# A graph network kernel on one core: distance factors of four batches at a time, with right sides made by a VectorE shuffle

## The chip, the cores and the metric

The kernel runs on one NeuronCore of one Trainium2 chip. The metric is the device time in microseconds (us) of one execution; the other cores are idle.

## The reference, cut to what matters

There are 16 batches of a graph with 512 nodes and 128 features. The first layer computes, for each batch, a convolution branch and a neighbour branch, and joins them in a GRU-like cell. The neighbour branch is where the change lies:

```python
s = x @ w_se.T + b_se                                  # 512 x 3
sq = jnp.sum(s * s, axis=-1)
dist = sq[:, :, None] + sq[:, None, :] - 2.0 * jnp.einsum('bnd,bmd->bnm', s, s)
A = jnp.exp(-dist) * mask
msg = jax.nn.relu(x @ w_msg.T + b_msg)
x_nmp = jnp.einsum('bnm,bmd->bnd', A, msg)
```

The convolution branch is a 1x1 convolution, a 17-tap convolution along the nodes and batch norms. A layer norm follows, then a small grouped graph layer over the first 32 nodes of each batch and a second layer norm.

## The kernel before, in words

One program handles one batch in each step, b = 0 to 15. Step 0 is unrolled with the loading of the weights (`first`), step 1 is unrolled, steps 2 to 13 are a loop over v = 2, 3, 4, 5 with four steps a turn, and steps 14 and 15 are unrolled. Odd and even steps differ: the convolution is done for two batches together, so its first half lies in the odd steps and its second half in the even ones. All five engines run their own instruction order, written out by hand, and meet at semaphores.

The negated distance matrix of a batch is a product of two thin factors. `rows` (TensorE, line 723 on) multiplies `wrow` by the inputs of two batches, one in the upper and one in the lower 64 partitions of the bank `p_gh`. From it ScalarE makes `ab` (`rows_factor`, L1016), VectorE makes `val` (`rows_val`, L1365), ScalarE rounds it (`rows_high`, L1020) and VectorE makes `left` (`rows_left`, L1369). For each of the two batches `left` holds 24 rows of the left factor and 24 rows of the right factor. This chain runs once in each odd step, for the two batches that come next, eight times in all.

The four 128-row pieces of a distance matrix are taken by four matrix products with 24 rows each (`dist`), which sit in four different groups of 32 partitions. The factors must therefore stand in all four groups. SyncE copies them there from SBUF to SBUF (`spread_factors`, L653 to L657): six transfers for each batch and twelve in an odd step, in one queue with the loads of `xin` (L680), the stores (L694) and the loads of `adj` (L626). The product of an even step uses the second batch of the pair, and that of the odd step the first one.

In an odd step VectorE runs in this order: `gate_mid`, `keep_share`, `result` (the end of the step before), `rows_val`, `mask_low` (`am_l`), `msg_sum`, `neighbour_steps`, `inner` (L1379), `rows_left`, `x_low` (L1361), `inner_low` (`t_l`, L1384), `second_steps`, `stats`, `outer`, `msg_low`, `neighbours_low`, `moments`, `middle_low`, `outer_low`, `first_sums`, and four `mask` (L1417). In the even step there follow the gates and `result` (L1434, L1436), `second_sums` (L1460 to L1462) and the rest. TensorE's fourth stream of the convolution (`stream(4, p_outer)`) waits for `second_sums`; `neighbours_low` (L1480) of the even step waits for TensorE's neighbour product through ScalarE (`neighbours`, L1062).

## Time and profile before

| quantity | value |
|---|---|
| median of 3 runs | 356.47 us (356.42 to 356.6) |
| profiled execution | 355.94 us |
| its span | 354.1 us |
| TensorE busy | 335.1 us (95%) |
| VectorE busy | 315.9 us (89%) |
| ScalarE busy | 237.4 us (67%) |
| mean granted TensorE clock | 0.99 of full speed |

The profile gives for each instruction its engine, its line, its start and its length, and for an engine that stood idle what ended the wait. PE is TensorE, DVE is VectorE, ACT is ScalarE, POOL is GpSimd, SPq is SyncE's queue. Two instructions of one engine may overlap a little, since one is filled while the one before drains.

### The profile page before, as it was taken

The numbers are of one execution on the slowest core, as the hardware profiler recorded it, in microseconds if no ns is written. First come the engines' busy times: TensorE is split into PE (matmuls) and PEld (weight loads), VectorE is DVE, ScalarE is ACT, GpSimd is POOL, SyncE is SP. The second block draws the span as 40 slices with busy tenths as digits, with TensorE's granted clock in tenths as the row PEclk, the third lists the DMA queues.
The fourth block names the chain that finished last, engine by engine and source line by source line (L and its number), as shares of the span: only waits on it lengthen the run. The fifth ranks groups of instructions, "written<-read, shape, count | busy, mean of one in ns | idle before, by whom it ended". The sixth has DMA issues, their size and how long they took to land. (4 is left out here: it accounts for less than half of the span.)

```text
span 354.1 us, 6242 instructions
## 1 busy us (share of the span) xinstructions
PE 335.1 (95%) x1769; PEld 273.2 (77%) x1769; DVE 315.9 (89%) x553; ACT 237.4 (67%) x409; POOL 94.4 (27%) x151
## 2 busy tenths in 40 slices
PE   5989999999999999999999999999999999999880
PEld 1577678987889688977998688968897798867570
DVE  2999999999999999999999999999999999896732
ACT  4382675748856696758674885669684886976760
POOL 4750001614050503231050506050222206052022
PEclk9999999999999999999999999999999999999996
DMA  6914331514153212604161404412260415301102
GB/s 197 310 23 126 103 118 47 168 31 149 24 145 109 99 52 64 210 0 148 39 205 30 148 17 109 149 67 81 56 203 15 148 33 156 107 26 37 30 2 60
DMA packets 31289, 34.01 MB, mean 96 GB/s; under 512 B 5111, under 2 KB 18463, under 8 KB 31271
## 3 DMA queue, kind: packets, MB, share of 16 engines
q1 hardware_dynamic: 30150, 33.49, 31.2%
q10 hardware_dynamic: 1120, 0.30, 0.4%
q8 instruction: 8, 0.13, 0.2%
q14 instruction: 11, 0.08, 0.1%
HBM read 24.85 MB, written 4.46 MB: 83 GB/s over the span
## 5 line engine op out<-in xcount | busy, mean ns | idle before, releaser
L1320 POOL TENSOR_TENSOR base<-mv,vscale 128x4 f32<-128x4 f32 x16 | 7.0, 437 | 230.9 <-DVE mv L1449 224.1
L715 PE MATMUL p_outer<-t_h,w_h 128*128 128x344 f32 x131 | 41.0, 328 | 0.0
L715 PE MATMUL p_outer<-t_h,w_l 128*128 128x344 f32 x131 | 40.3, 322 | 0.5 <-DVE w_l L1527 0.5
L1417 DVE TENSOR_TENSOR am<-am,adj 128x512 f32<-128x512 f32 x64 | 39.8, 682 | 0.0
L1583 DVE TENSOR_TENSOR am_l<-am,am_h 128x2048 fp32r<-128x2048 f32 x15 | 34.3, 2287 | 1.8 <-ACT am_h L1172 1.8
L715 PE MATMUL p_middle<-t_h,w_h 128*128 128x344 f32 x90 | 28.6, 329 | 0.6 <-DVE rz L1533 0.6
L1172 ACT ACTIVATE am_h<-am 128x2048 fp32r<-128x2048 f32 x15 | 28.5, 1901 | 0.0
L715 PE MATMUL p_middle<-t_h,w_l 128*128 128x344 f32 x90 | 28.0, 322 | 0.0
L715 PEld LDWEIGHTS p_outer<-t_h,w_h 128*128 128x128 f32 x131 | 24.3, 188 | 2.1 <-ACT t_h L1029 0.4
L1131 ACT ACTIVATE yoo<-yn,nb,rs 128x128 f32<-128x128 f32 x63 | 25.9, 483 | 0.0
L715 PEld LDWEIGHTS p_outer<-t_h,w_l 128*128 128x128 f32 x131 | 24.4, 189 | 1.1 <-DVE w_l L1527 0.8
L715 PE MATMUL ring<-am_h,m_h 128*128 128x512 f32 x60 | 24.2, 404 | 0.6 <-DVE mt L1406 0.6
L715 PE MATMUL p_outer<-t_l,w_h 128*128 128x344 f32 x131 | 24.7, 322 | 0.0
L1062 ACT ACTIVATE n_h<-ring 128x512 fp32r<-128x512 f32 x16 | 9.5, 596 | 22.2 <-PE ring L715 22.2
L715 PE MATMUL ring<-am_h,m_l 128*128 128x512 f32 x60 | 23.5, 392 | 0.0
L1076 ACT ACTIVATE gtn<-gtn,vec 128x512 f32<-128x512 f32 x15 | 10.9, 724 | 17.6 <-DVE gtn L1423 17.6
L1329 POOL TENSOR_TENSOR nmr<-mv,rs 128x4 f32<-128x4 f32 x16 | 21.1, 1322 | 2.7 <-issue 0.9
L715 PEld LDWEIGHTS p_outer<-t_l,w_h 128*128 128x128 f32 x131 | 21.6, 188 | 0.0
L1327 POOL TENSOR_TENSOR rs<-base,cst 128x5 f32<-128x5 f32 x16 | 21.0, 1314 | 1.3
L715 PEld LDWEIGHTS p_middle<-t_h,w_h 128*128 128x128 f32 x90 | 16.8, 189 | 0.8 <-issue 0.8
L1049 ACT ACTIVATE am<-p_outer 128x512 f32<-128x512 f32 x14 | 8.4, 599 | 12.9 <-PE p_gh L715 12.9
L715 PE MATMUL p_middle<-t_l,w_h 128*128 128x344 f32 x90 | 16.9, 322 | 0.0
(381 smaller groups left out, 1012.1 us busy)
## 6 DMA issues: line engine op xcount, KB each, us to landing
adj<-adjT SPq DMA_DIRECT2D x64, 256.0 KB, 3.4
xpad<-xT SPq DMA_DIRECT2D x17, 256.0 KB, 3.1
out<-yoo SPq DMA_DIRECT2D x16, 256.0 KB, 2.3
crossed<-left SPq DMA_DIRECT2D x31, 48.0 KB
left<-left SPq DMA_DIRECT2D x30, 48.0 KB
right<-left SPq DMA_DIRECT2D x30, 48.0 KB
wc<-w_c SPq DMA_DIRECT2D x2, 384.0 KB, 6.8
wraw<-g_w SPq DMA_DIRECT2D x1, 640.0 KB
```

The lines of the kernel that those rows point to most:

```text
L715: return nc.tensor.matmul(out_, w, x, start=start, stop=stop, skip_group_check=True)
L1049: A(am[:, c, :], banks[c][:], ACT.Exp).then_inc(s_e[c], 1)
L1062: A(n_h[:], R_NMP[:], ACT.Copy).then_inc(s_nh, 1)
L1076: A(nn, tt, ACT.Tanh, bias=vec[:, V_IN:V_IN + 1]).then_inc(s_nn, 1)
L1131: return A(yo[q][:, c, :], rows_, ACT.Identity, bias=nb[:, c:c + 1], scale=rs[:, c:c + 1])
L1172: A(am_h[:], am[:], ACT.Copy).then_inc(s_amh, 1)
L1320: TT(base[:, 0:CH], mv[:, :, 1], vscale[:, 0:CH], ALU.mult)
L1327: TT(rs[:], base[:], cst[:, C_MH:C_MH + CH + 1], ALU.pow).then_inc(s_rs, 1)
L1329: TT(nmr[:, 0:CH], mv[:, :, 0], rs[:, 0:CH], ALU.mult)
L1417: TT(am[:, c, :], am[:, c, :], adj[:, c, :], ALU.mult).then_inc(s_am[c], 1)
L1583: TT(am_l[:], am[:], full(am_h[:]), ALU.subtract).then_inc(s_aml, 1)
```

## The change

The factors get 30 rows of 15 and 15, so that both sides of a batch lie in one group of 32 partitions, the right side being the left one with its halves exchanged. One chain now makes the factors of up to four batches: batches 0 and 1 at the start, 2 and 3 in step 1, and 4 to 7, 8 to 11 and 12 to 15 in steps 3, 7 and 11. For the last two batches of such a group TensorE reads a copy `xr` of the inputs, loaded by SyncE in the steps with v = 2. In steps 5, 9 and 13 the chain is gone. The right sides are made by a `stream_shuffle` on VectorE, which writes `crossed` behind `x_low`. SyncE spreads seven transfers for each batch into `lefts` and `rights`, which exist twice: fourteen in steps 1, 3, 7 and 11, and seven in each of the steps with v = 4 and v = 5. In the start the right side of batch 0 is copied by ScalarE, and the bias column `brow` comes in one transfer.

The core of the diff:

```diff
-KD = 24
+KROW = 15
+KD = 2 * KROW
...
-            left.append((k, 1.0, 0.0, low))
-            right.append((None, 0.0, -1.0, 0))
-    for low in (0, 1):
-        for k in range(3):
-            left.append((None, 0.0, 1.0, 0))
-            right.append((k, -1.0, 0.0, low))
-    return left, right
+    first, second = [], []
+    for k in range(3):
+        first += [(k, 0.0, 1.0, 0), (k, 0.0, 1.0, 0), (k, 0.0, 1.0, 1), (k, -1.0, 0.0, 0), (k, -1.0, 0.0, 1)]
+        second += [(k, 0.0, 1.0, 0), (k, 0.0, 2.0, 1), (k, 0.0, 1.0, 1), (None, 0.0, 1.0, 0), (None, 0.0, 1.0, 0)]
+    return first + second, []
...
@@ -148,8 +140,9 @@
         adj = sb("adj", [128, CH, N])
         rows2 = sb("rows2", [128, 2 * N]); ab = rows2[:, 0:N]; val = rows2[:, N:2 * N]; val_h = sb("val_h", [128, N], fp32r)
-        left = sb("left", [128, N], fp32r)
-        crossed = sb("crossed", [128, N], fp32r); left2 = sb("left2", [128, N], fp32r); right2 = sb("right2", [128, N], fp32r)
+        left = sb("left", [128, N], fp32r); crossed = val
+        lefts = [sb(f"lefts{p}", [128, N], fp32r) for p in range(2)]; rights = [sb(f"rights{p}", [128, N], fp32r) for p in range(2)]
+        xr = sb("xr", [128, 2, N])
         he = sb("he", [128, 2, 2 * W3 + 2])
...
-                rows_l, rows_r = full(left[64 * q:64 * q + KD, :]), full(left[64 * q + 32:64 * q + 32 + KD, :])
-                sp.dma_start(full(crossed[64 * q:64 * q + KD, :]), rows_r).then_inc(s_right[q], 16)
-                sp.dma_start(full(crossed[64 * q + 32:64 * q + 32 + KD, :]), rows_l).then_inc(s_right[q], 16)
-                for at in (64 - 64 * q, 96 - 64 * q):
-                    sp.dma_start(full(left2[at:at + KD, :]), rows_l).then_inc(s_right[q], 16)
-                    sp.dma_start(full(right2[at:at + KD, :]), rows_r).then_inc(s_right[q], 16)
+            def spread_factors(v, event=None):
+                g, p = v % 4, v % 2
+                rows_l, rows_r = full(left[32 * g:32 * g + KD, :]), crossed[32 * g:32 * g + KD]
+                for h in range(4):
+                    if h != g:
+                        sp.dma_start(full(lefts[p][32 * h:32 * h + KD, :]), rows_l).then_inc(s_right[p], 16)
+                if event is not None:
+                    after(sp, s_crossed, event)
+                for h in range(4):
+                    sp.dma_start(full(rights[p][32 * h:32 * h + KD, :]), rows_r).then_inc(s_right[p], 16)
             sp.wait_ge(s_left, 1)
-            sp.dma_start(full(crossed[0:KD, :]), full(left[32:32 + KD, :])).then_inc(s_right[0], 16)
-            spread_factors(1)
+            spread_factors(1, 1)
             sp.wait_ge(s_zero, 3)
             for g, q in itertools.product(range(NG), range(2)):
                 load_group(g, q)
...
                     sp.dma_start(xin[:, (v + 3) % 4, :], xT[(b + 3) % B, :, :]).then_inc(s_x[(v + 3) % 4], 16)
-                if v % 2 and before(b, B - 2):
-                    after(sp, s_left, n.pair(1))
+                if v == 2:
+                    after(sp, s_rows, n.quad(0))
                     for q in range(2):
-                        spread_factors(q)
+                        sp.dma_start(xr[:, q, :], xT[b + 4 + q, :, :]).then_inc(s_xr, 16)
+                if v == 3 or static(b, 1):
+                    after(sp, s_left, n.quad(0)); after(sp, s_d, n(1))
+                    spread_factors(v + 1, n.quad(0))
+                    spread_factors(v + 2)
+                elif not isinstance(b, int):
+                    if v != 2:
+                        after(sp, s_d, n(0))
+                        spread_factors(v + 2)
                 if not static(b, 1):
...
-            def rows(v):
+            def row_group(g, x_):
+                return mm(p_gh[32 * g:32 * g + 32, :], wrow[:], x_)
+            def rows(v, extra=False):
                 for q in range(2):
-                    last = mm(p_gh[64 * q:64 * q + 64, :], wrow[:], xin[:, (v + q) % 4, :])
+                    last = row_group((v + q) % 4, xin[:, (v + q) % 4, :])
+                if extra:
+                    for q in range(2):
+                        last = row_group(2 + q, xr[:, q, :])
                 last.then_inc(s_rows, 1)
...
-                at, other = 64 * (v % 2), 64 - 64 * (v % 2)
-                for c, (lhs, rhs, row) in enumerate(((left, crossed, at), (crossed, left, at + 32),
-                                                     (left2, right2, other), (left2, right2, other + 32))):
-                    last = mm(banks[c][:], lhs[row:row + KD, D * c:D * c + D], rhs[row:row + KD, :])
+                for c in range(CH):
+                    h, p = (v + c) % 4, v % 2
+                    lhs, rhs = left if c == 0 else lefts[p], rights[p]
+                    last = mm(banks[c][:], lhs[32 * h:32 * h + KD, D * c:D * c + D], rhs[32 * h:32 * h + KD, :])
                 last.then_inc(s_d, 1)
...
                         pe.wait_ge(s_x[(v + k) % 4], x_count(n, v, k))
-                    after(pe, s_ghb, n(0))
-                    rows(v + 1)
+                    if v == 3 or static(b, 1):
+                        after(pe, s_ghb, n(0))
+                        if v == 3:
+                            after(pe, s_xr, n.quad(-2) * 32)
+                        rows(v + 1, v == 3)
                     after(pe, s_xh, n(3)); after(pe, s_xl, n(3))
                     after(pe, s_w0, n.pair(0)); after(pe, s_pq, n.pair(0)); after(pe, s_e[0], n(1))
                     conv1(q, p_middle)
...
                     g_pe.combine(pe, mm)
-                if more:
-                    after(pe, s_val, n.pair(1))
+                if v == 3 or static(b, 1):
+                    after(pe, s_val, n.quad(0))
                 after(pe, s_ghb, n(0)); gate(p_gh, "n", 2, xb_h, xb_l, True, True).then_inc(s_gx, 1)
                 turn(n)
...
                 if more:
-                    after(pe, s_left, n.pair(1)); after(pe, s_right[0], n.pair(1) * 96 - 80)
+                    after(pe, s_left, n.quad(0)); after(pe, s_right[0], n.pair(0) * 112)
...
-            def rows_high(n, k):
-                after(act, s_val, n.pair(k + 1)); after(act, s_left, n.pair(k))
-                A(val_h[:], val, ACT.Copy).then_inc(s_valh, 1)
+            def rows_factor(at, e):
+                after(act, s_rows, e); after(act, s_val, e - 1)
+                A(ab[at], p_gh[at, :], ACT.Identity, bias=rowb[at, 0:1], scale=cst[at, C_ROW:C_ROW + 1]).then_inc(s_ab, 1)
+            def rows_high(at, e):
+                after(act, s_val, e); after(act, s_left, e - 1)
+                A(val_h[at, :], val[at], ACT.Copy).then_inc(s_valh, 1)
             def first_conv(n, k, slot, source):
                 after(act, s_c1, n(k + 1)); after(act, s_f, n.pair(0))
...
                 act.dma_start(vec[:], vecs[:, :]).then_inc(s_vec, 16)
-                act.dma_start(wrow[:], w_rows[:, :]).then_inc(s_wrowd, 16)
+                act.dma_start(wrow[:], w_rows[:, 0:32]).then_inc(s_wrowd, 16)
                 act.dma_start(wmsg[:], w_msg[:, :]).then_inc(s_wmsgd, 16)
-                for q in range(2):
-                    act.dma_start(brow[64 * q:64 * q + 64, :], b_rows[:, :]).then_inc(s_brow, 16)
+                act.dma_start(brow[:], b_rows[0:32, :].unsqueeze(0).broadcast_to([4, 32, 1])).then_inc(s_brow, 16)
                 act.dma_start(bmsg[:], b_msg[:, :].to_broadcast([128, D])).then_inc(s_bmsg, 16)
...
                 act.wait_ge(s_rowb, 1)
-                act.wait_ge(s_rows, 1)
-                A(ab, p_gh[:], ACT.Identity, bias=rowb[:, 0:1], scale=cst[:, C_ROW:C_ROW + 1]).then_inc(s_ab, 1)
-                act.wait_ge(s_val, 1)
-                A(val_h[:], val, ACT.Copy).then_inc(s_valh, 1)
+                rows_factor(slice(0, 64), 1)
+                rows_high(slice(0, 64), 1)
                 middle_high(o)
                 act.wait_ge(s_mt, 1)
                 A(m0, mt[:], ACT.Relu).then_inc(s_m0, 1)
+                act.wait_ge(s_crossed, 1)
+                A(rights[0][0:32, :], crossed[0:32], ACT.Copy).then_inc(s_cross0, 1)
                 act.wait_ge(s_wsum, 2)
                 A(w3_h[:], u3, ACT.Copy).then_inc(s_whi, 1)
...
-            def rows_val(n, k):
-                after(dve, s_ab, n.pair(k + 1)); after(dve, s_valh, n.pair(k))
-                STT(val, p_gh[:], brow[:, 0:1], ab, ALU.add, ALU.mult).then_inc(s_val, 1)
-            def rows_left(n, k):
-                after(dve, s_valh, n.pair(k + 1)); after(dve, s_d, n(2 * k + 1))
-                STT(left[:], full(val_h[:]), cst[:, C_ROW + 2:C_ROW + 3], val, ALU.mult, ALU.add).then_inc(s_left, 1)
+            def rows_val(at, e, done):
+                after(dve, s_ab, e); after(dve, s_valh, e - 1); after(dve, s_d, done)
+                STT(val[at], p_gh[at, :], brow[at, 0:1], ab[at], ALU.add, ALU.mult).then_inc(s_val, 1)
+            def rows_left(at, e, done):
+                after(dve, s_valh, e); after(dve, s_d, done)
+                STT(left[at, :], full(val_h[at, :]), cst[at, C_ROW + 2:C_ROW + 3], val[at], ALU.mult, ALU.add).then_inc(s_left, 1)
+            def rows_crossed(at, e):
+                nc.vector.stream_shuffle(crossed[at], full(left[at, :]), MIRROR).then_inc(s_crossed, 1)
             def neighbour_steps(n):
...
                 last.then_inc(s_t04, 1)
-                rows_val(o, 0)
-                rows_left(o, 0)
+                rows_val(slice(0, 64), 1, 0)
+                rows_left(slice(0, 64), 1, 0)
+                dve.wait_ge(s_left, 1)
+                rows_crossed(slice(0, 64), 1)
                 dve.wait_ge(s_bmsg, 16)
                 msg_sum(z, 0, FIRST_MSG)
                 dve.wait_ge(s_w2d[1], 16)
...
                     neighbour_steps(n)
                     inner(n)
-                    rows_left(n, 0)
+                    if v == 3 or static(b, 1):
+                        rows_left(part_of(v), n.quad(0), n(1))
+                        after(dve, s_left, n.quad(0))
                     x_low(v, n, 3)
+                    if v == 3 or static(b, 1):
+                        rows_crossed(part_of(v), n.quad(0))
                     inner_low(n)
                     second_steps(n)
                 else:
```

## Rows read from the trace of the kernel before

**Rows 1.** The page, part 1: busy time of each engine over the span.

```profile
PE 335.1 (95%) x1769; PEld 273.2 (77%) x1769; DVE 315.9 (89%) x553; ACT 237.4 (67%) x409; POOL 94.4 (27%) x151
```

**Rows 2.** One period: window, length, busy PE, PEld, DVE, ACT, POOL, clock, DMA share.

```profile
100.00:138.72 38.72, 38.66 (x211) 32.55 (x207) 37.03 (x63) 27.75 (x45) 9.76 (x15) 1.00 0.32 98
```

**Rows 3.** Timeline of VectorE, step 7 into step 8 (start us, length us).

```profile
169.69 0.75 DVE L1369 SCALAR_TENSOR_TENSOR left<-val_h,cst,rows 128x512 fp32r<-128x512 f32 x1
170.35 0.69 DVE L1361 TENSOR_TENSOR x_l<-xpad,x_h 128x512 fp32r<-128x512 f32 x1
170.96 0.90 DVE L1384 TENSOR_TENSOR t_l<-yy,t_h 128x712 fp32r<-128x712 f32 x1
...
178.69 2.48 DVE L1417 TENSOR_TENSOR am<-am,adj 128x512 f32<-128x512 f32 x4
...
183.28 0.69 DVE L1434 SCALAR_TENSOR_TENSOR yy<-rz,gtn 128x512 f32<-128x512 f32 x1 [0.19 <-ACT gtn L1076]
184.07 0.69 DVE L1436 TENSOR_TENSOR yy<-yy 128x512 f32<-128x512 f32 x1
...
185.65 0.57 DVE L1462 SCALAR_TENSOR_TENSOR wc<-p_outer,prm,wc 128x344 f32<-128x344 f32 x1
```

**Rows 4.** Timeline of TensorE at the fourth stream of step 8.

```profile
185.94 0.60 PE L794 MATMUL ring<-cst,yy 128*128 128x128 f32 x4
186.29 0.41 PE L715 MATMUL p_outer<-t_h,w_h 128*128 128x344 f32 x1
```

**Rows 5.** Timeline of VectorE in step 4, where a neighbour product is read.

```profile
115.10 0.69 DVE L1480 TENSOR_TENSOR n_l<-ring,n_h 128x512 fp32r<-128x512 f32 x1 [0.52 <-ACT n_h L1062]
```

**Rows 6.** Timeline of TensorE at the row products of step 5.

```profile
121.38 1.08 PE L715 MATMUL p_gh<-xpad,wrow 128*64 128x512 f32 x4
122.39 0.51 PE L715 MATMUL p_middle<-x_h,wc_h 128*128 128x512 f32 x1
```

**Rows 7.** Timelines of step 5: ScalarE, VectorE and TensorE, a line each.

```profile
122.74 0.72 ACT L1076 ACTIVATE gtn<-gtn,vec 128x512 f32<-128x512 f32 x1 [0.56 <-DVE gtn L1423]
123.37 0.76 ACT L1016 ACTIVATE rows<-p_gh,rowb,cst 128x512 f32<-128x512 f32 x1
124.03 1.90 ACT L1172 ACTIVATE am_h<-am 128x2048 fp32r<-128x2048 f32 x1
...
131.09 0.80 ACT L1029 ACTIVATE t_h<-yy 128x712 fp32r<-128x712 f32 x1
...
125.96 2.29 DVE L1583 TENSOR_TENSOR am_l<-am,am_h 128x2048 fp32r<-128x2048 f32 x1
...
129.93 1.13 DVE L1379 SCALAR_TENSOR_TENSOR yy<-he 128x712 f32<-128x712 f32 x1
...
132.25 0.89 DVE L1384 TENSOR_TENSOR t_l<-yy,t_h 128x712 fp32r<-128x712 f32 x1
...
132.15 0.32 PE L715 MATMUL p_outer<-t_h,w_h 128*128 128x344 f32 x1
```

**Rows 8.** A small VectorE instruction of the start.

```profile
40.86 0.15 DVE L1571 TENSOR_SCALAR dg<-dg 106x8 f32<-106x8 f32 x1
```

**Rows 9.** Step 5: SyncE's queue, the DMA engines by stretch, TensorE at the distances.

```profile
135.60 0.71 SPq L657 DMA_DIRECT2D right<-left  x1
136.36 0.71 SPq L653 DMA_DIRECT2D crossed<-left  x1
...
137.00:137.20 0.20, 0.20 (x3) 0.20 (x2) 0.20 (x1) 0.10 (x1) 0.00 (x0) 1.00 0.72 174
...
138.45 0.50 PE L715 MATMUL p_outer<-crossed,left 24*128 24x512 f32 x1
```

**Rows 10.** Timelines of the start: ScalarE, VectorE, TensorE.

```profile
18.10 0.85 ACT L1101 ACTIVATE w_h<-gtn 128x768 fp32r<-128x768 f32 x1 [3.61 <-DVE gtn L1520]
...
22.38 0.96 DVE L1530 TENSOR_TENSOR w_l<-gtn,w_h 128x768 fp32r<-128x768 f32 x1 [0.23 <-ACT w_h L1106]
...
24.89 1.20 PE L715 MATMUL p_middle<-t_h,w_h 128*128 128x344 f32 x6 [0.64 <-DVE rz L1533]
```

More of the change, by code:

```diff
@@ L86, in constants @@
     c[:, C_ID:C_ID + D] = np.eye(D)
-    for side, rows in enumerate(dist_rows()):
-        for r, (_, alpha, beta, low) in enumerate(rows):
-            for b in range(2):
-                c[64 * b + 32 * side + r, C_ROW:C_ROW + 3] = alpha, beta, -low
+    for r, (_, alpha, beta, low) in enumerate(dist_rows()[0]):
+        for g in range(4):
+            c[32 * g + r, C_ROW:C_ROW + 3] = alpha, beta, -low
     c[:, C_ONE] = 1
@@ L1609, in odd @@
                 result(n, -1)
-                if more:
-                    rows_val(n, 0)
+                if v == 3 or static(b, 1):
+                    rows_val(part_of(v), n.quad(0), n(1))
                 if not more:
```

41 lines of the change are left out of this document (20 added, 21 removed).

## The prediction

> **What bounds the kernel now.** I read the page first. TensorE is busy for 95% of the span and VectorE for 89% [rows 1], so TensorE looks like the bound, and a change that takes work from TensorE looks like a gain. The busy time by stretch corrects this. In one period of two steps, 38.72 us, TensorE is busy for 38.66 us and VectorE for 37.03 us [rows 2]. VectorE has 1.7 us left in a period, and part of that are gaps that a dependent instruction leaves behind itself. Both engines are full.
>
> The timelines then show which of the two holds the other, and where. From the writing of `left` in step 7 to the last of `second_sums` in step 8, VectorE's instructions follow each other without a wait for TensorE; the only named wait is 0.19 us for ScalarE, which itself follows from VectorE [rows 3]. The last `second_sums` starts at 185.65 and ends at 186.22. TensorE has its four transposes at 185.94, which take 0.35 us from start to start, and begins its fourth stream at 186.29 [rows 4]. That stream waits for `second_sums`, so VectorE is on time there by less than 0.1 us. What VectorE gets later before that place, TensorE gets later too. In the other direction VectorE waits 0.52 us for the neighbour product of the even step [rows 5]. There the clocks of the two are set together again, so a reserve that VectorE has won before it isn't carried past it. The bound is a loop through both: VectorE from the even step's neighbour product to `second_sums`, and TensorE from there to the next neighbour product.
>
> **The change part by part.**
>
> *TensorE, removed.* The row products occupy TensorE from 121.38 to 122.39, 1.0 us [rows 6]. Eight groups become five: steps 5, 9 and 13 lose theirs, so TensorE has 3 x 1.0 = 3.0 us less to do. In steps 3, 7 and 11 four products of 32 columns stand where two of 64 stood. A product has two records here, and 4 records are done in 1.08 us, so two column groups run beside each other; I take four to do the same, at no cost. The upper bound is that only two do: 1.0 us more in three steps.
>
> *The distance products.* 30 rows instead of 24 in the same four row groups: no cost, since the columns stay at 512.
>
> *Steps 5, 9 and 13, what the gain is worth.* The chain into the first stream of the odd step is: the candidate's tanh at 122.74, `ab` at 123.37, `am_h` at 124.03 on ScalarE, `am_l` at 125.96 on VectorE as soon as `am_h` is done, `inner` at 129.93, `t_h` at 131.09 to 131.89, TensorE at 132.15 [rows 7]. Without `ab`, `am_h` can start when the tanh ends, at 123.46: 0.57 us earlier. `rows_val` lies under `am_h` and gives nothing more. So `t_h` ends at 131.32, and TensorE, which would be ready 1.0 us earlier, at 131.15, starts at about 131.35: it gains 0.8 us. VectorE also drops `left`, and its `t_l` moves from 132.25 to the end of `t_h`, 0.9 us, so it isn't what limits here. Value: 0.8 us for each of the three; bounds 0.57 (only the chain's part) and 1.0 (all of TensorE's). Sum: -2.4 us, between -1.7 and -3.0.
>
> *Steps 1, 3, 7 and 11, what VectorE gets.* All of the old chain stays, and two things are added on VectorE between `left` and `t_l`: a wait for `left`'s own semaphore ahead of `x_low`, and the shuffle. `x_low` now starts 0.09 us before `left` has ended [rows 3]. A dependent pair with a wait starts 0.10 us after the end of the first (L1434 and L1436 in the same rows), so the wait costs up to 0.2 us; I take 0.15, and the lower bound is 0. The trace has no shuffle. The nearest row is `x_low`, also 512 elements a partition in fp32, with 0.61 us from start to start; `left` has 0.66. The shuffle's permutation must be loaded as well, by a small instruction; a small instruction of VectorE takes 0.15 us [rows 8], of which some may be overlapped. I take 0.70 us for both, between 0.60 and 0.95. Together 0.85 us, between 0.60 and 1.15. The Trainium skill, VectorE: DVE Perf Modes, section The DRAIN you can't avoid, says that a semaphore between two VectorE instructions costs nothing extra; the rows above show 0.2 us between the two cases, and by the rule the sum of this prediction would be about 0.8 us instead of 1.6. The same page, section The perf-mode tier table, gives a shuffle about 2400 ns for 2048 elements in its only mode, from which 512 elements would be an estimated 0.60 us.
>
> Nothing covers these 0.85 us. Behind them stand `t_l`, the steps of the convolution, four masks at 178.69, the gates and `second_sums`, each at once behind the other [rows 3], and TensorE's fourth stream has no reserve [rows 4]. So each of the four periods gets 0.85 us longer: +3.4 us, between +2.4 and +4.6. `t_l` itself is still just in time for TensorE.
>
> *The start.* The same wait and shuffle stand in `first`, ahead of the sums of the taps, for which ScalarE waits 3.61 us; the later VectorE work there holds TensorE, which waits 0.64 us at 24.89 [rows 10]. One wait of VectorE for ScalarE, 0.23 us, takes up a part. Cost +0.6 us of 0.85, between 0.35 and 0.9. ScalarE's copy of batch 0's right side lies in those 3.61 us. The bias column comes in one transfer instead of two; I give it nothing.
>
> *SyncE's transfers.* One starts 0.76 us after the other. The sixth, the last one that the odd step's product waits for, starts at 135.60, the DMA engines still move data for it from 137.0 to 137.2 and I take 137.4 as its end, and TensorE takes the factors at 138.45 [rows 9]. With 0.76 us more the seventh lands at about 138.1, 0.3 us in time. The four right sides wait for the shuffle, but three left sides are issued first, 2.3 us, and the shuffle is done about 1.5 us after `left`. Behind the fourteen transfers stand the store and the `adj` loads of the step, later by two transfers, 1.5 us, and their masks stand a whole step further on; in the steps with v = 4 and 5 the seven transfers stand in an idle queue. Cost nothing; if the queue's cover is gone, see the rival.
>
> Sum: +0.6 + 3.4 - 2.4 = +1.6 us. The profiled execution took 355.94 us with a span of 354.1, and would take 357.5; the median of the runs lies 0.53 us above it, so 356.47 + 1.6 = 358.1 us.
>
> **The rivals.** 0.2% is 0.7 us, and that is about what a measurement can tell from no change.
>
> *VectorE's additions are cheap.* The shuffle and the wait cost 0.60 us, 0.35 in the start, and steps 5, 9 and 13 give 0.9 each: 0.35 + 2.4 - 2.7 = 0.05 us, no change, 356.5 us. For it: `x_low`'s own 0.61 us. Against it: the gap behind a wait. Chance 22%.
>
> *TensorE alone sets the time.* If VectorE has a reserve of 0.85 us before `second_sums` that I don't see, its additions are hidden and the 3.0 us stand: 353.5 us. For it: 95% against 89% [rows 1]. Against it: under 0.1 us between the engines at the fourth stream. It decides once the reserve is above the cost of the additions. Chance 13%.
>
> *The right sides come late.* If a transfer of 30 rows costs more of SyncE's queue than one of 24, the seventh lands later. In proportion to the rows it would be 0.95 us each; the seventh would land at about 139.3 and hold TensorE by 0.85 us, beside VectorE's delay and not on top of it. It decides above that: at 1.15 us each, TensorE is 2.05 us late, 1.2 us more than VectorE, four times: 358.1 + 4.8 = 362.9 us. Chance 7%.
>
> *The four narrow products don't run together.* TensorE is 1.0 us later in three steps; 0.85 us of it lie beside VectorE's delay, so it adds 0.15 x 3: 358.6 us. Chance 8%. The Trainium skill, TensorEngine Tiling (Array Packing), section Tiling Modes, counts four independent tiles of 128x32, which speaks against this rival; only the two column groups are seen here.
>
> **How the numbers follow.** My forecast has 50%. Its own range is 356.9 to 359.6, from the bounds of the additions and of the gain. Slower by over 0.2%: most of the forecast (45%), late right sides and serial products: 60%. Within 0.2%: the cheap additions and the low end of the forecast: 24%. Faster: TensorE alone and the best end of the cheap case: 16%. The range of 8 in 10 is 355.1 to 359.8: it leaves out TensorE alone and most of the late right sides.
>
> **What would show it.** In the profile after, VectorE's `t_l` in step 7 starts about 0.85 us later behind `left` than 1.27 us, and `second_sums` ends after TensorE's transposes, with TensorE waiting about 0.8 us there in steps 2, 4, 8 and 12. The period with step 5 is 0.8 us shorter, with TensorE's first stream waiting for `t_h`. The row products of step 7 take 1.0 us. I am wrong if the fourth stream starts right behind the transposes in step 8, if the shuffle takes clearly more or less than 0.7 us, or if TensorE waits at the distances of step 3.

## The result, and the profile after

The kernel after takes 364.38 us (median of 4 runs) against 356.45 us before; the ratio is 1.0154, with an interval of 1.0084 to 1.0225. Here and below the medians are over all executions, while the ratios leave disturbed ones out. I had forecast 358.1 us and a range up to 359.8. The direction was right, the time lies outside the range. The profiled execution took 363.85 us with a span of 362.0, 7.9 us more than before.

The page of the kernel after, first the busy time [rows 1], then two rows of the 40 slices:

```profile
PE 335.5 (93%) x1769; PEld 273.5 (76%) x1769; DVE 316.8 (88%) x557; ACT 234.6 (65%) x404; POOL 91.0 (25%) x151
...
PE   4498998999998999999999999999999999999880
...
PEclk9789999999999999999999999999999999999996
```

TensorE's busy time is the same (335.1 us before) although it has less to do. Its first two slices have lost time (4 and 4 tenths, 5 and 9 before), while the third is nearly full, and the granted clock fell to 7 and 8 tenths in the second and third (9, which is 90% or more, before). To place the rest I took, in both traces, the start of each batch's four distance products on TensorE. Their differences are the delay so far:

| stretch, from which products to which | after minus before, us | forecast |
|---|---|---|
| span's start to batch 0 (25.05 for 18.34) | +6.7 | +0.6 |
| batch 0 to 1 | +0.04 | (in the row above) |
| batch 1 to 3, with step 1 | +1.53 | +0.85 |
| batch 3 to 5, with step 3 | +1.53 | +0.85 |
| batch 5 to 7, with step 5 | -0.91 | -0.8 |
| batch 7 to 9, with step 7 | +0.83 | +0.85 |
| batch 9 to 11, with step 9 | -0.92 | -0.8 |
| batch 11 to 13, with step 11 | +0.81 | +0.85 |
| batch 13 to 15, with step 13 | -0.99 | -0.8 |

The middle came out nearly as forecast. The start did not, and steps 1 and 3 cost nearly twice what I gave them. At batch 15 the delay is 8.6 us, of which the span keeps 7.9: from there to the end the kernel after takes 42.4 us and the one before 43.2, and no run shows why.

**The start.** VectorE, GpSimd and TensorE of the kernel after, timelines (start us, length us):

```profile
10.71 0.27 DVE L1533 TENSOR_SCALAR rowb<-brow,cst 128x1 f32<-128x1 f32 x1 [3.31 <-DMA brow<-b_rows]
10.90 0.70 DVE L1537 TENSOR_TENSOR he<-he 128x534 f32<-128x534 f32 x1
11.64 0.63 DVE L1540 SCALAR_TENSOR_TENSOR yy<-he 128x356 f32<-128x356 f32 x1
12.19 2.05 DVE L1537 TENSOR_TENSOR he<-he 128x534 f32<-128x534 f32 x1
14.27 2.12 DVE L1540 SCALAR_TENSOR_TENSOR yy<-he 128x356 f32<-128x356 f32 x1
...
12.05 1.61 POOL L1329 TENSOR_TENSOR yoo<-wc 128x640 f32<-128x640 f32 x1 [4.02 <-DMA wc<-w_c]
13.74 2.15 POOL L1331 TENSOR_TENSOR gtn<-yoo,wc 128x768 f32<-128x768 f32 x1
...
16.44 5.78 PE L731 MATMUL p_outer<-yy,wc 128*128 128x344 f32 x12 [4.98 <-DVE yy L1540]
```

For comparison, VectorE and TensorE of the kernel before:

```profile
8.25 0.27 DVE L1504 TENSOR_SCALAR rowb<-brow,cst 128x1 f32<-128x1 f32 x1 [0.56 <-DMA brow<-b_rows]
...
11.17 3.75 PE L715 MATMUL p_outer<-yy,wc 128*128 128x344 f32 x12 [0.42 <-DVE yy L1511]
...
18.34 0.70 PE L715 MATMUL ring<-crossed,left 24*128 24x512 f32 x2 [0.53 <-issue]
```

The bias column `brow`, now one transfer, lets VectorE wait 3.31 us for a tiny instruction, and everything of the start is queued behind it. Of two equal pairs of `he` and `yy`, the convolution's first terms, the first takes 0.70 and 0.63 us, the second, beside GpSimd's tap sums, 2.05 and 2.12. TensorE stands idle for 4.98 us. Then its twelve products take 5.78 us where they took 3.75 before. The windows of the kernel after show the clock over this time (window, length, busy PE, PEld, DVE, ACT, POOL, granted clock, DMA share):

```profile
11.00:14.00 3.00, 0.47 (x5) 0.28 (x3) 2.97 (x3) 0.77 (x1) 1.87 (x2) 0.96 1.04 391
14.00:16.40 2.40, 0.00 (x0) 0.00 (x0) 2.37 (x3) 0.00 (x0) 2.32 (x2) 0.50 0.75 279
16.40:18.00 1.60, 1.56 (x3) 1.08 (x4) 0.90 (x2) 0.92 (x2) 1.60 (x1) 0.50 0.11 42
...
19.50:20.50 1.00, 1.00 (x3) 0.65 (x2) 1.00 (x2) 0.53 (x1) 0.93 (x1) 0.50 0.23 55
20.50:22.00 1.50, 1.50 (x6) 0.94 (x5) 1.47 (x3) 0.92 (x3) 0.86 (x2) 0.97 0.23 55
```

While TensorE is idle the clock goes from 2.4 to 1.2 GHz (0.50 of full speed) and stays there until about 20.5. The 6.7 us are therefore, to 0.1 us, 2.46 for the column (10.71 instead of 8.25), 2.81 for the slow pair, 2.03 for the slow products, less 0.53 that TensorE had idle ahead of its first distance products before.

**Step 7.** VectorE [rows 3] and SyncE's queue [rows 9] of the kernel after, and TensorE at the distance products:

```profile
178.62 0.74 DVE L1394 SCALAR_TENSOR_TENSOR left<-val_h,cst,rows 128x512 fp32r<-128x512 f32 x1
179.48 0.69 DVE L1386 TENSOR_TENSOR x_l<-xpad,x_h 128x512 fp32r<-128x512 f32 x1
180.10 0.01 DVE L1398 LOAD_MASK_SELECT rows<-left  x1
180.10 0.74 DVE L1398 STREAM_SHUFFLE rows<-left 128x512 f32<-128x512 f32 x1
180.73 0.89 DVE L1413 TENSOR_TENSOR t_l<-yy,t_h 128x712 fp32r<-128x712 f32 x1
...
179.38 2.52 SPq L662 DMA_DIRECT2D lefts<-left  x3
181.94 3.25 SPq L666 DMA_DIRECT2D rights<-rows  x4
...
186.74 0.47 PE L731 MATMUL p_outer<-rights,left 30*128 30x512 f32 x1 [0.51 <-issue]
...
195.39 0.57 DVE L1491 SCALAR_TENSOR_TENSOR wc<-p_outer,prm,wc 128x344 f32<-128x344 f32 x1
...
196.01 0.43 PE L731 MATMUL p_outer<-t_h,w_h 128*128 128x344 f32 x1
```

and TensorE at the same distance products of the kernel before:

```profile
177.13 0.50 PE L715 MATMUL p_outer<-crossed,left 24*128 24x512 f32 x1
```

From `left` to `t_l` 2.11 us pass instead of 1.27. The 0.84 us more are 0.63 for the shuffle, start to start, and 0.20 for the wait ahead of `x_low` (0.86 from `left` to `x_l`, 0.66 before); loading the permutation takes 0.01. That is the term as I sized it. But the row at 186.74 is a second finding: TensorE stood idle for 0.51 us ahead of the distance products, a wait that the profile gives only as "issue". They start 8.12 us after `left`; before they started 7.44 us after it (177.13 after 169.69), and TensorE was never idle there. And in step 8 `second_sums` ends at 195.96 and TensorE starts its fourth stream at 196.01, right behind transposes at 195.57. I had written that this would make me wrong: the wait of 0.8 us for VectorE isn't there, since TensorE is late already. So would a wait of TensorE at the distances of step 3, and there the idle time is larger still:

```profile
109.54 0.47 PE L731 MATMUL p_outer<-rights,left 30*128 30x512 f32 x1 [1.38 <-issue]
```

**Steps 5 and 7, what was removed.** TensorE's row products in step 7 [rows 6], and the first stream of step 5 [rows 7], of the kernel after:

```profile
168.97 0.62 PE L731 MATMUL p_gh<-xpad,wrow 128*32 128x512 f32 x2
168.99 0.62 PE L731 MATMUL p_gh<-xr,wrow 128*32 128x512 f32 x2
169.43 0.60 PE L731 MATMUL p_gh<-xpad,wrow 128*32 128x512 f32 x2
169.44 0.60 PE L731 MATMUL p_gh<-xr,wrow 128*32 128x512 f32 x2
169.97 0.50 PE L731 MATMUL p_middle<-x_h,wc_h 128*128 128x512 f32 x1
...
140.26 0.80 ACT L1054 ACTIVATE t_h<-yy 128x712 fp32r<-128x712 f32 x1 [0.60 <-DVE yy L1408]
...
141.11 0.19 PEld L731 LDWEIGHTS p_outer<-t_h,w_h 128*128 128x128 f32 x1 [0.43 <-ACT t_h L1054]
141.11 0.43 PE L731 MATMUL p_outer<-t_h,w_h 128*128 128x344 f32 x1
```

The four narrow products run beside each other and take 1.0 us together, as the two did. In step 5 the first stream starts as soon as `t_h` is done at 141.06; its weight load (PEld) had waited 0.43 us for `t_h`, so the chain through ScalarE limits there, as forecast.

### The profile page after: what moved, and what is told of

The parts are those of the page before. It is cut to its first block and busy times, and to the rows that moved or that the text cites. A ratio compares the mean times of both kernels' runs of the same rounds, so it can differ in the third digit from the quotient of the medians.

```text
span 362.0 us, 6268 instructions
## 1 busy us (share of the span) xinstructions
PE 335.5 (93%) x1769; PEld 273.5 (76%) x1769; DVE 316.8 (88%) x557; ACT 234.6 (65%) x404; POOL 91.0 (25%) x151
## 5 line engine op out<-in xcount | busy, mean ns | idle before, releaser
L1354 POOL TENSOR_TENSOR nmr<-mv,rs 128x4 f32<-128x4 f32 x16 | 19.8, 1235 | 2.7 <-issue 0.9
```

The source lines that it names most:

```text
L1354: TT(nmr[:, 0:CH], mv[:, :, 0], rs[:, 0:CH], ALU.mult)
```

## The experiments

All were compared with the kernel before on the same chip. In the table, "step 7" is the stretch from batch 7's distance products to batch 9's in the profiled execution, less the 38.55 us of the kernel before; "left to dist" is from the start of `left` in step 7 to batch 8's distance products. The column "start to batch 0" is read from one execution of each kernel. It differs by 2 us among kernels whose column came in time (17.31 to 19.29), for a reason given at c2.

| kernel | median, us | ratio to before | start to batch 0 | step 7 | left to dist |
|---|---|---|---|---|---|
| before | 356.5 to 356.9 | 1 | 18.34 | 0 | 7.44 |
| after | 364.38 | 1.0154 (1.0084 to 1.0225) | 25.05 | +0.83 | 8.12 |
| a1, two brow transfers | 356.90 | 1.0019 (0.9987 to 1.0051) | 17.78 | +0.83 | 8.12 |
| b1, before with one | 363.67 | 1.0172 (1.0125 to 1.0218) | 24.20 | +0.02 | |
| b2, b1 issued early | 359.32 | 1.0034 (0.9999 to 1.0068) | 21.76 | | |
| c3, b1 without the repeat | 362.15 | 1.0117 (1.0072 to 1.0163) | 24.86 | | |
| c2, b1 with GpSimd held | 360.27 | 1.0088 (1.0057 to 1.0119) | 22.08 | | |
| c1, after, rowb later | 358.80 | 1.0057 (1.0018 to 1.0097) | 17.02 | +0.84 | |
| a3, wait covered | 357.81 | 1.0036 (1.0013 to 1.0059) | 18.00 | +0.69 | 8.12 |
| a4, six transfers | 357.36 | 1.0017 (0.9994 to 1.0040) | 19.00 | +0.86 | 7.70 |
| d1, no shuffle | 356.44 | 0.9996 (0.9960 to 1.0032) | 17.62 | +0.68 | 8.13 |
| g1, no shuffle, six | 354.07 | 0.9926 (0.9904 to 0.9948) | 17.31 | -0.01 | 7.39 |
| g2, wait covered, six | 356.68 | 0.9999 (0.9979 to 1.0019) | 19.29 | +0.61 | 7.45 |
| f1, halves by SyncE | 354.95 | 0.9955 (0.9938 to 0.9971) | 19.18 | +0.16 | 7.39 |

### The bias column

**a1.** The kernel after with the column's loading of before.

```diff
-act.dma_start(brow[:], b_rows[0:32, :].unsqueeze(0).broadcast_to([4, 32, 1])).then_inc(s_brow, 16)
+for q in range(2):
+    act.dma_start(brow[64 * q:64 * q + 64, :], b_rows[:, :]).then_inc(s_brow, 16)
```

> The kernel after, with the bias column brow loaded in two transfers of 64 rows as before, and nothing else. Theory 1, the single broadcast transfer lands late and the whole start slides behind it: VectorE's rowb starts again near 8.3 us with a wait of about 0.9, its he and yy take 0.7 and 0.6 instead of 2.05 and 2.12, the first distance products start near 19.0 to 19.4 (before 18.34, after 25.05), and the kernel takes 358 to 359 us. Rival, the start is late because of the shuffle, the copy of batch 0's right side and the changed order there, and the transfer is only another thing to wait for: the first distance products stay above 23 us and the kernel takes 363 to 364 us.

Measured: 356.90 us, no difference from before that can be told, and the first distance products at 17.78 us. The rival falls: shuffle, ScalarE's copy and the new order of the start cost nothing up to batch 0's products; at batch 1's this kernel is 0.55 us behind the one before. The time, 1 to 2 us under what I expected, also says that the rest of the change is nearer to no change than to my +1.6.

**b1.** The kernel before with one transfer of the column.

```diff
-for q in range(2):
-    act.dma_start(brow[64 * q:64 * q + 64, :], b_rows[:, :]).then_inc(s_brow, 16)
+act.dma_start(brow[:], b_rows[:, :].unsqueeze(0).broadcast_to([2, 64, 1])).then_inc(s_brow, 16)
```

> The kernel before, with brow loaded by one transfer that repeats 64 rows twice, and nothing else. Theory 1: the start alone gets longer, the first distance products at 22 to 25 us instead of 18.34, and the kernel takes 360 to 363 us. Rival, the transfer is harmless: within 0.3 us of the kernel before. If the distance products are late by the lateness of rowb alone (about 2.5 us), and VectorE's he and yy keep their 0.7 and 0.6 us, then what made them 1.4 us longer each in the kernel after was not this transfer.

Measured: 363.67 us. All batches from the first to the last are 5.9 us late (5.86 at batch 0, 5.91 at batch 15), so the column alone, without anything else of the change, gives a start as late as that of the kernel after, to 0.85 us. VectorE and TensorE of b1:

```profile
10.49 0.27 DVE L1503 TENSOR_SCALAR rowb<-brow,cst 128x1 f32<-128x1 f32 x1 [3.09 <-DMA brow<-b_rows]
...
12.71 1.97 DVE L1510 SCALAR_TENSOR_TENSOR yy<-he 128x356 f32<-128x356 f32 x1
...
14.74 6.64 PE L715 MATMUL p_outer<-yy,wc 128*128 128x344 f32 x12 [3.42 <-DVE yy L1510]
```

The column is late by 2.24 us, one slow `yy` adds 1.33, and the products at the lower clock 2.89. Taken the other way, from the kernel after to a1, the column gives 7.3 us at batch 0, 6.7 at batch 15 and 7.5 in the medians.

**c2.** b1, and GpSimd waits.

```diff
 nc.gpsimd.tensor_copy(u2[:, G3 - 1:G3, :], wc2[:, TAPS - 2:TAPS - 1, :])
+pool.wait_ge(s_t04, 1)
```

> b1_one_brow, with GpSimd's tap sums held until VectorE's second yy is done. In b1_one_brow the second yy took 1.97 us instead of 0.63, beside GpSimd's first sum. Theory, the two slow each other: yy takes 0.63 again, and TensorE's p_outer<-yy starts 1.3 us earlier, at 13.4 instead of 14.74; the kernel is 1 to 2 us shorter than b1_one_brow if the later tap sums hold nobody. Rival, yy was slow for another reason (late data, the DMA engines): it keeps its 1.97 us. If TensorE's idle time of 3.42 us, now about 2.1, is also what its granted clock fell after (0.69 in the stretch from 10 to 20 us), the twelve products that took 6.64 us instead of 3.75 get shorter as well.

Measured: 360.27 us. In this run `rowb` itself came later (11.08 for 10.49), and yet TensorE began earlier:

```profile
11.08 0.27 DVE L1504 TENSOR_SCALAR rowb<-brow,cst 128x1 f32<-128x1 f32 x1 [3.68 <-DMA brow<-b_rows]
...
13.30 0.63 DVE L1511 SCALAR_TENSOR_TENSOR yy<-he 128x356 f32<-128x356 f32 x1
...
13.99 5.27 PE L715 MATMUL p_outer<-yy,wc 128*128 128x344 f32 x12 [2.73 <-DVE yy L1511]
```

`yy` takes 0.63 us with GpSimd standing still, so what made b1's `yy` slow is contention between the two engines. The products took 5.27 us instead of 6.64, after a shorter idle time. The span is 1.9 us shorter than that of b1, within the 1 to 2 us expected.

Which of the two starts first decides. GpSimd's first tap sum starts when its operand `wc`, the convolution's weights, has landed, at another time in each execution. In a4, where the column came in time (8.26), it did so ahead of `yy`:

```profile
10.09 1.79 POOL L1337 TENSOR_TENSOR yoo<-wc 128x640 f32<-128x640 f32 x1 [1.76 <-DMA wc<-w_c]
...
10.52 1.85 DVE L1548 SCALAR_TENSOR_TENSOR yy<-he 128x356 f32<-128x356 f32 x1
```

The same holds over all fourteen traces: the `he` or `yy` that starts 0.05 to 0.55 us behind a GpSimd sum takes 1.85 to 2.12 us, and a `yy` that starts 0.18 us or more ahead of it keeps its 0.63 to 0.64. In a4, f1 and g2 `yy` came second, and their batch 0 stands at 19.0 to 19.3 us instead of 17.3 to 18.3. So the slow pair is not a fixed price of the late column; the late column moved `he` and `yy` behind GpSimd's start.

**c1.** The kernel after, one transfer, but `rowb` and its wait behind the two pairs of `he` and `yy`.

```diff
-dve.wait_ge(s_brow, 16); dve.wait_ge(s_cst, 16)
-TS(rowb[:], brow[:], cst[:, C_ROW:C_ROW + 1], cst[:, C_ROW + 1:C_ROW + 2], ALU.mult, ALU.add).then_inc(s_rowb, 1)
...
 last.then_inc(s_t04, 1)
+dve.wait_ge(s_brow, 16); dve.wait_ge(s_cst, 16)
+TS(rowb[:], brow[:], cst[:, C_ROW:C_ROW + 1], cst[:, C_ROW + 1:C_ROW + 2], ALU.mult, ALU.add).then_inc(s_rowb, 1)
```

> The kernel after, with its single broadcast transfer of brow kept, but VectorE's rowb and the wait for brow moved behind the two he and yy, so that the late column no longer stands ahead of them in VectorE's queue. Theory 1, the late column costs what it does only because VectorE's queue stands still behind it: yy's end returns to about 10.9 us, TensorE starts p_outer<-yy near 11.2 instead of 16.44, the first distance products start at 18.5 to 19.5 us, and the kernel takes 357 to 358.5 us. Rival, the late values of the row products themselves hold the start: the first distance products stay above 22 us and the kernel takes over 361.

Measured: 358.80 us, and the first distance products at 17.02 us, earlier than in any other kernel. The late column costs what it does because an in-order queue stands behind it; it is not needed itself until later. By batch 1 c1 is 0.87 us behind the kernel before. The median lies 0.3 us above what I expected. The profiled execution took 362.18 us: the granted clock was 0.55 from 340 to 350 us, and the part behind batch 15's products took 46.7 us instead of the 42.5 of a1, so those 4 us say nothing about the column.

**c3 and b2.** What makes the one transfer late? c3 is the kernel before with one transfer of 128 rows from a column of 128 values, b2 is b1 with the transfer issued right behind `vec`.

```diff
-for q in range(2):
-    act.dma_start(brow[64 * q:64 * q + 64, :], b_rows[:, :]).then_inc(s_brow, 16)
+act.dma_start(brow[:], b_rows[:, :]).then_inc(s_brow, 16)
```

```diff
+act.dma_start(brow[:], b_rows[:, :].unsqueeze(0).broadcast_to([2, 64, 1])).then_inc(s_brow, 16)
 act.dma_start(wrow[:], w_rows[:, :]).then_inc(s_wrowd, 16)
 act.dma_start(wmsg[:], w_msg[:, :]).then_inc(s_wmsgd, 16)
-act.dma_start(brow[:], b_rows[:, :].unsqueeze(0).broadcast_to([2, 64, 1])).then_inc(s_brow, 16)
```

> The kernel before, with brow loaded by one plain transfer of 128 rows from a column of 128 values, so without the repeat. Theory, what delays the column is one transfer of 128 rows of 4 bytes where two of 64 stood: rowb waits about 3.1 us as in b1_one_brow and the kernel takes 360 to 364 us. Rival, the repeat in the source delays it: rowb waits 0.6 us, and the time is that of the kernel before.

> b1_one_brow, with the one broadcast transfer of brow issued second on ScalarE's queue, right behind vec (at about 1.2 us instead of 2.14), ahead of wrow and wmsg. In b1_one_brow the column was there at 10.4 us, 8.3 us after its issue. If such a transfer has a long time of its own, it lands about 8 us after its issue again, rowb starts near 9.5 us, and the kernel takes 360 to 362 us. Rival, it is late because it meets the loads of the weights and of x on the same DMA engines, and issued ahead of them it finds the engines free: rowb starts at 8.3 us or before, and the kernel takes 356.5 to 357.5 us.

Measured: 362.15 and 359.32 us. In c3 the first distance products start at 24.86, as late as with the repeat, but `rowb` now waits last for the transfer of `cst`, the constants that SyncE loads:

```profile
10.45 0.27 DVE L1503 TENSOR_SCALAR rowb<-brow,cst 128x1 f32<-128x1 f32 x1 [3.54 <-DMA cst<-consts]
```

`cst` took 7.8 us from issue to landing, 5.4 before, and `brow` 6.7 us, where the two took 4.7 and 5.5. In b2 `rowb` starts at 9.37, close to the 9.5 of a transfer with a long time of its own, but again it is `cst` that came last. b2's time lies between the two that I had expected. So taking the repeat away does not bring the start back, although the column itself was there sooner after its issue (6.7 us for 8.3 in b1), and an earlier place in the queue gets back about 1.1 us of VectorE's wait. `cst` was late as well in c3, b2 and b1 (7.8, 6.6 and 6.0 us), but not in c2 and in the kernel after (5.3). Why one transfer of 128 four-byte rows is late, and at times its neighbour, no run shows; this stays open.

### VectorE's additions and the transfers

**a3.** a1 with the wait and the shuffle later.

```diff
 rows_left(part_of(v), n.quad(0), n(1))
-after(dve, s_left, n.quad(0))
 x_low(v, n, 3)
-rows_crossed(part_of(v), n.quad(0))
+after(dve, s_left, n.quad(0))
 inner_low(n)
+rows_crossed(part_of(v), n.quad(0))
```

> a1_two_brow with VectorE's wait for its own left, and the shuffle, moved behind x_low and inner_low in steps 1, 3, 7 and 11, so that two other instructions cover the wait. Theory 2, VectorE's additions cost 0.63 us for the shuffle and 0.2 us for the wait ahead of it, and both delay second_sums: from left's start to t_l's start 1.9 us instead of 2.1 and the kernel 0.4 to 0.8 us shorter than a1_two_brow. Rival, in these steps the right sides' transfers decide: they start 1.2 us later here, so steps 1 and 3 get longer by up to 1.2 us each, and the kernel is 0.5 to 2 us longer than a1_two_brow.

Measured: 357.81 us, 1.0036; against a1 no gain can be told in the medians. In the profile step 7 costs 0.69 us instead of 0.83, and the distance products still come 8.12 us after `left`. The rival did not come true: the transfers started no later, because three left sides cover the later shuffle.

**a4.** a1 with ScalarE writing the own group's right side, six transfers instead of seven.

```diff
 for h in range(4):
-    sp.dma_start(full(rights[p][32 * h:32 * h + KD, :]), rows_r).then_inc(s_right[p], 16)
+    if own or h != g:
+        sp.dma_start(full(rights[p][32 * h:32 * h + KD, :]), rows_r).then_inc(s_right[p], 16)
...
+A(rights[0][g:g + 32, :], crossed[g:g + 32], ACT.Copy).then_inc(s_cross0, 1)
```

> a1_two_brow, where in steps 1, 3, 7 and 11 ScalarE copies the right side of the batch's own row group in place of one of the seven SyncE transfers, so that six transfers stand ahead of the odd step's distance products. Theory 3, the seventh transfer lands late where TensorE stood idle before the distance products (1.38 us in step 3, 0.51 in step 7): steps 1 and 3 get 0.5 to 0.8 us shorter each, steps 7 and 11 stay, and the kernel is 1 to 1.6 us shorter than a1_two_brow. Rival, the seventh transfer is hidden and ScalarE's copy of about 0.7 us lies in the way: the same time or up to 1 us more.

Measured: 357.36 us, no gain over a1 where I had expected 1 to 1.6 us. TensorE's idle time ahead of the distance products is gone in all four steps (7.68 to 7.74 us after `left`), but only step 3 got shorter, from +1.37 in a1 to +0.82; step 7 kept +0.86. As an explanation of the whole, theory 3 falls.

**d1.** a1 without the shuffle and its wait (an excerpt; the transfers of the right sides read rows that the shuffle of the start has written, from a buffer of their own).

```diff
-after(dve, s_left, n.quad(0))
 x_low(v, n, 3)
-rows_crossed(part_of(v), n.quad(0))
```

> a1_two_brow without the shuffle and without the wait ahead of it in steps 1, 3, 7 and 11; the right sides of every later batch are copies of the first shuffle's rows, so this kernel leaves out the mirroring and computes other distances. SyncE has the same fourteen transfers, and they wait only for left. Theory 2, VectorE's additions cost about 0.83 us in each of these four steps and hide nothing: 3 to 3.5 us shorter than a1_two_brow, 353.5 to 354 us, and steps 1 and 3 lose their extra 0.3 to 0.5 us as well because the right sides leave earlier. Rival, the transfers decide in these steps: only 1 us shorter or less. If the whole comes to less than 2.8 us shorter than the kernel before, something else in the change costs too.

Measured: 356.44 us; I had expected 353.5 to 354. This was the run that overturned my account: VectorE has 0.83 us less to do in each of four steps, and step 7 still costs 0.68. VectorE, SyncE and TensorE of d1:

```profile
171.17 0.75 DVE L1395 SCALAR_TENSOR_TENSOR left<-val_h,cst,rows 128x512 fp32r<-128x512 f32 x1
...
172.43 0.90 DVE L1414 TENSOR_TENSOR t_l<-yy,t_h 128x712 fp32r<-128x712 f32 x1
...
171.94 2.52 SPq L662 DMA_DIRECT2D lefts<-left  x3
174.50 3.25 SPq L666 DMA_DIRECT2D rights<-crossed  x4
...
179.30 0.47 PE L731 MATMUL p_outer<-rights,left 30*128 30x512 f32 x1 [0.63 <-issue]
```

`left` to `t_l` is 1.26 us again, but the seven transfers leave `left` as late as ever, and the distance products come 8.13 us after it. Seven transfers give 8.12 or 8.13 in step 7 of after, a1, a3 and d1 alike, whatever VectorE does. The kernel before needs 7.44; the difference, 0.68, is what the step costs in d1.

**g1.** So there are two delays side by side. g1 takes both away: d1 with a4's copy.

> d1_no_shuffle and a4_own_right together: no shuffle and no wait on VectorE in steps 1, 3, 7 and 11 (the mirroring is left out, the right sides are copies of the first shuffle's rows), and ScalarE writes the own group's right side, so that six transfers stand ahead of the odd step's distance products. Revised theory: two delays of about the same size lie side by side in each of these steps, VectorE's additions (0.83 us) and the seventh transfer with its larger pieces (the distance products start 8.12 us after left in every kernel with seven transfers, 7.44 before the change), and the later one counts; taking away one gives little, both together give 0.7 to 0.8 us a step: the distance products start 7.4 to 7.5 us after left, the kernel takes 353 to 354 us, about 3 us less than the kernel before. Rival, there is a third thing that costs in these steps: no better than d1_no_shuffle, 356.4 us.

Measured: 354.07 us, ratio 0.9926. Step 7 costs nothing (-0.01) and the distance products start 7.39 us after `left`. Over both kinds of periods: the removed row products give 0.89 us in step 5, and steps 7 and 11 take back nothing. Only step 3 still waits, 0.84 us for its right sides:

```profile
101.21 0.50 PE L732 MATMUL p_outer<-rights,left 30*128 30x512 f32 x1 [0.84 <-DMA rights<-crossed]
```

**g2.** a3 and a4 together, the whole computation.

> a3_late_wait and a4_own_right together: the whole computation, with the wait for left covered, the shuffle behind inner_low, and six transfers ahead of the odd step's distance products. By the revised theory VectorE's 0.63 us of the shuffle alone stay: each of the four steps costs 0.63 to 0.68 instead of 0.83, so 0.6 to 0.8 us less than a1_two_brow, 356.0 to 356.5 us, the time of the kernel before. Rival, the transfers of the right sides, which now leave 0.8 us later, still land last: the time of a1_two_brow or more, with TensorE idle ahead of the distance products.

Measured: 356.68 us, ratio 0.9999 (0.9979 to 1.0019). With the transfers in time only the shuffle itself is left: steps 3, 7 and 11 cost 0.58, 0.61 and 0.58 us (at a granted clock of 1.00; in this execution it fell only from 330 us on), against a gain of three times 0.9. Step 1 still costs 1.54.

**f1.** The whole computation, with neither: SyncE crosses the halves, and the urgent batch uses two row groups.

```diff
-for h in range(4):
-    sp.dma_start(full(rights[p][32 * h:32 * h + KD, :]), rows_r).then_inc(s_right[p], 16)
+for h in (g, (g + 1) % 4) if near else range(4):
+    for a, z in ((0, KROW), (KROW, 0)):
+        sp.dma_start(full(rights[p][32 * h + a:32 * h + a + KROW, :]),
+                     full(left[32 * g + z:32 * g + z + KROW, :])).then_inc(s_right[p], 16)
...
-for c in range(CH):
-    h, p = (v + c) % 4, v % 2
+for c in (0, 2, 1, 3) if near else range(CH):
+    h, p = (v + (c // 2 if near else c)) % 4, v % 2
```

> The whole computation without the shuffle in steps 1, 3, 7 and 11: SyncE crosses the rows itself, with two transfers of 15 rows for each right side, and the batch whose products come in the same step uses two row groups instead of four, so that five transfers (one left side, four halves) stand ahead of them; its four distance products then run in two pairs. TensorE gets 0.25 us more in four steps, VectorE nothing. If a transfer of 15 rows takes about 0.67 us of the queue, the five are issued in 3.5 us and land early. Then each of the four steps costs 0.25 us instead of 0.83 and steps 5, 9 and 13 keep their 0.9: 354 to 355 us, faster than both kernels. Rival, the small transfers cost as much as the large ones or more: eleven for each later batch fill SyncE's queue (9 us of each step), the loads of adj come late, and the kernel takes 357 us or more.

Measured: 354.95 us, ratio 0.9955 (0.9938 to 0.9971): 0.45% faster than the kernel before. SyncE and TensorE of f1 in step 7:

```profile
171.68 0.89 SPq L662 DMA_DIRECT2D lefts<-left  x1
172.62 3.25 SPq L670 DMA_DIRECT2D rights<-left  x4
...
178.38 6.54 SPq L670 DMA_DIRECT2D rights<-left  x8
...
178.30 0.49 PE L735 MATMUL p_outer<-rights,left 30*128 30x512 f32 x1
...
178.63 0.39 PE L735 MATMUL ring<-rights,left 30*128 30x512 f32 x1
```

The five urgent transfers are issued by 175.87 and land ahead of TensorE; the second pair of products starts 0.33 us behind the first, and step 7 costs 0.16 us. A transfer of 15 rows takes the queue 0.82 us, not the 0.67 I expected: as much as one of 30. Eleven of them for each later batch still found room.

## Why the prediction was wrong

*"The bias column comes in one transfer instead of two; I give it nothing."* This is the step that failed, and it is worth 5.9 of the 7.9 us (b1), or 6.7 when it is taken out of the kernel after (a1). I looked at the number of transfers and not at what waits for them: VectorE already waited 0.56 us for the column before, with the convolution's first terms queued behind that wait, so there was no cover at all. Then two costs came on top that no row of the change's own operations shows: contention with GpSimd, behind whose start VectorE's `he` and `yy` had slid, and the lower clock after TensorE's idle time. Without this term even the bounds, added up plainly, end at 360.3 us (356.47 + 0.9 + 4.6 - 1.7; the low end is 356.2, so the range 356.9 to 359.6 is narrower than its own bounds).

*The start otherwise, +0.6.* Not resolved. The start is the same in a1, a3, a4 and g2, and batch 1's products come 0.55 us late in a1, where the clock fell between 21 and 24 us, 0.03 us in a3, where it did not, and 0.66 and 0.96 us in a4 and g2, where `yy` began behind GpSimd. At batch 3 the four are 1.44 to 1.67 us behind, whatever they were at batch 1, and the forecast for the start and step 1 together was 1.45.

*VectorE's additions, 0.85 us.* Measured 0.84, 0.63 and 0.20 of it for shuffle and wait. The reasoning that nothing covers them was right in its sum and incomplete in its cause. The rule of the Trainium skill, VectorE: DVE Perf Modes, section The DRAIN you can't avoid, that a semaphore between two VectorE instructions costs nothing extra, would have left the 0.20 out; the trace does not agree (0.86 us with the wait, 0.66 without), and covering the wait in a3 took 0.14 us off step 7.

*SyncE's transfers, "0.3 us in time", cost nothing.* Wrong, the second step that failed. The seventh decides when TensorE takes the factors, 0.68 us later than before. This is the rival "the right sides come late", to which I gave 7%. Two sizes were off. A transfer takes 0.82 to 0.86 us of the queue, not 0.76, so the seventh's issue starts 5.78 us after `left` instead of 5.37; and from there to the distance products pass 2.34 us, where I had taken 1.8 us for the landing, read from when the DMA engines were busy [rows 9]; the trace of the kernel after gives 2.1 to 2.2 us from issue to landing in step 7. That is 0.95 us, and with 0.29 us of it in reserve 0.66 are left, the 0.68 measured. I had priced that rival as something that adds nothing until it passes VectorE's delay, and this held: in step 7 it lies beside VectorE's delay, and the longer one counts. In step 3 it does pass: the distance products wait until 9.02 us after `left` (8.86 in a1), the step costs 1.53 instead of 0.83, and a4, with one transfer less, brings it back to 0.82. In that step one of the right sides took 3.0 us from issue to landing in the kernel after, 2.8 in a1 and 3.2 in g1, and none more than 2.2 in a4; what held it is open. Step 1 costs 1.53 in the kernel after, 1.17 in a1, 1.57 in a4, 1.54 in g2 and 0.31 in g1. Since batch 3 is as late in a4 as in a1, part of these differences is only where the start's delay is counted, and a split of step 1 isn't shown.

*Steps 5, 9 and 13, -0.8 each.* Measured -0.91, -0.92 and -0.99. The chain through `am_h`, `inner` and `t_h` is the limit, as written. From the candidate's tanh to the start of `t_h` it got 0.65 us shorter (7.70 for 8.35), where I had 0.57, and TensorE takes `t_h` 0.05 us after its end instead of 0.26.

*The rivals.* TensorE alone sets the time: refuted, since with six transfers VectorE's additions are worth 0.87 us in step 7 (a4 against g1). The narrow products: refuted, 1.0 us. Cheap additions: refuted by 0.84 us, although with the column repaired the result, 356.90, is near that of this rival, 356.5. The profile of a1 adds up otherwise: 0.55 + 1.17 + 1.37 + 0.83 + 0.82 for the start and steps 1, 3, 7 and 11 of a1, less 0.89, 0.87 and 1.01, is 1.97 at batch 15, of which the span keeps 1.3 us, while the medians, 356.90 against 356.71, differ by 0.2, which can't be told from nothing.

## What to carry to other kernels

Before an edit to a load is costed at nothing, find the first instruction that waits for it and read what is queued behind that wait, even if the transfer has 512 bytes; and let a small instruction that waits for a late load stand behind the work that doesn't need it. Where taking away a cost changes nothing, look for a second delay of the same size beside it, and measure from a common event (here `left`) to the consumer: a constant distance over kernels that differ elsewhere names the path. Two engines that start by their own loads can fall into another order when one load moves, and the order alone was worth 1.2 to 1.3 us for one instruction here. An "issue" wait ahead of a product whose operands come by DMA was, in this case, the DMA.

## What the runs showed of the hardware

- Two VectorE instructions of 534 and 356 elements took 2.05 and 2.12 us beside GpSimd's `TENSOR_TENSOR`, 0.70 and 0.63 without it (after), and `yy` went from 1.97 to 0.63 us when GpSimd was held (b1, c2). The one that started second was slow: `yy` took 1.85 us when it started 0.43 us behind GpSimd (a4) and 0.63 when it started 0.24 us ahead of it (before).
- The granted clock went to 1.2 GHz while TensorE stood idle for 4.98 us and stayed there up to 20.5 us, 4 us after it had resumed. Over the stretch from 10 to 20 us it was 1.00, 0.83, 0.69 and 0.69 for idle times of 0.42, 2.73, 3.42 and 4.98 us ahead of the first stream (before, c2, b1, after). But it was 0.83 after 1.84 us (b2) and 1.00 after 2.39 us (a4), and in a1 it also fell to 0.50 from 21 to 24 us, behind gaps of 0.39 and 0.60 us, and in d1, with the same gaps, it did not; a gap alone doesn't foretell it.
- A copy from SBUF to SBUF takes SyncE's queue 0.82 us for 15 rows of 2 KB (f1) and for 30 rows (after), and 0.76 us for 24 (before): here the number of transfers counts, hardly their size.
- One transfer of 128 rows of 4 bytes was there 8.3 us after its issue (b1) and 6.7 us without the repeat in its source (c3), two of 64 rows after 4.7 and 5.5 us (before).
